# Another order of TensorE's calls in one step of a strided-attention kernel

## The reference, cut to what matters

```python
xn = layernorm(x)                                   # x: 4 x 2048 x 256, float32
q, k, v = heads(xn @ q_w), heads(xn @ k_w), heads(xn @ v_w)      # 16 heads of 16
q = q * sigmoid(unity_scale)
scores = q @ k.T / sqrt(16)
allowed = (j % 4 == 0) | (abs(i - j) <= 8)          # key j for query i
attn = softmax(where(allowed, scores, -inf))
linear = fp8_round(xn) @ weight_fp8.T + bias
out = x + (attn @ v) @ o_w + o_b + linear
```

## Time and profile before

| | us |
|---|---|
| median of 3 runs | 1435.28 (1432.79 to 1437.56) |
| profiled execution | 1432.67 |
| its span, first to last instruction | 1430.9 |
| TensorE busy | 1333.4 (93%) |
| VectorE busy | 1072.3 (75%) |
| ScalarE busy | 824.4 (58%) |
| GpSimd busy | 265.6 (19%) |
| steps with units and scores, 343.03 to 1306.12 | 963.1 |

### The profile page before, as it was taken

How to read it: one execution, slowest core, us unless ns; L and a number is a source line. 1 busy time by engine, 2 the same in 40 slices (tenths; PEclk the granted TensorE clock), 3 DMA queues, 4 the chain that set the end, 5 groups by cost and what they waited for, 6 DMA issues and landing times.

```text
span 1430.9 us, 29098 instructions
## 1 busy us (share of the span) xinstructions
PE 1333.4 (93%) x9792; PEld 635.7 (44%) x9792; DVE 1072.3 (75%) x2583; ACT 824.4 (58%) x1524; POOL 265.6 (19%) x382
## 2 busy tenths in 40 slices
PE   6689888979999999999999999999999999999996
PEld 3466666623434334434334443444344344444385
DVE  7999999777777777767767776777677777777222
ACT  2333333306777667767666776767677667776800
POOL 5543333420111111111111111111111111111100
PEclk9899999958999999999999999999999999999998
DMA  5566666962354444435353544444353525443258
GB/s 179 166 182 182 176 189 196 236 147 41 95 109 102 100 103 110 107 92 103 96 106 92 111 103 97 100 103 109 95 108 95 109 88 117 103 101 94 71 175 289
DMA packets 209060, 178.08 MB, mean 124 GB/s; under 512 B 49808, under 2 KB 185616, under 8 KB 207376
## 3 DMA queue, kind: packets, MB, share of 16 engines
q1 hardware_dynamic: 201168, 168.20, 46.2%
q10 hardware_dynamic: 7744, 7.87, 1.7%
HBM read 106.93 MB, written 69.07 MB: 123 GB/s over the span
## 4 chain that ended last, share of the span: by engine, by line
PE 64%; DMA 10%; issue 2%; ACT 1%; DVE 1%; ACTq 0%; POOL 0%; DVEq 0%; POOLq 0%
PE ps_attend L919 17%; PE ps_attend L934 15%; PE ps_attend L895 15%; DMA q_op<-negmax_dram 9%; PE ps_attend L941 5%; PE ps_attend L903 3%; PE ps_attend L900 3%; PE ps_attend L976 3%; PE ps_attend L920 3%; ACT probs L813 1%; DVE masked L866 1%; DMA q_op<-attn_dram 1%; PE ps_attend L892 1%; ACT out_rows L785 0%; ACT probs L818 0%
## 5 line engine op out<-in xcount | busy, mean ns | idle before, releaser
L866 DVE CUSTOM_DVE_ANT_0 masked<-ps_attend,max_mask 128x620 bf16<-128x620 f32 x1024 | 774.5, 801 | 255.5 <-PE ps_attend L920 252.2
L813 ACT ACTIVATE probs<-ps_attend 128x512 f32<-128x512 f32 x1024 | 572.3, 600 | 280.2 <-PE ps_attend L895 278.7
L919 PE MATMUL ps_attend<-k_op,q_op 96*128 96x512 bf16 x1024 | 404.7, 395 | 26.3 <-issue 15.3
L895 PE MATMUL ps_attend<-q_op,k_op 99*128 99x512 bf16 x1024 | 393.2, 386 | 9.6 <-DMA q_op<-negmax_dram 6.2
L934 PE MATMUL ps_attend<-probs,v_op 128*32 128x512 f32 x2048 | 275.8, 611 | 0.1
L919 PEld LDWEIGHTS ps_attend<-k_op,q_op 96*128 96x128 bf16 x1024 | 100.2, 98 | 298.4 <-DVE peak L866 254.8
L920 PE MATMUL ps_attend<-k_op,q_op 96*128 96x108 bf16 x1024 | 219.0, 214 | 0.0
L690 POOL CAST negmax<-peak 128x16 bf16<-128x16 f32 x64 | 12.6, 196 | 887.9 <-DVE peak L866 887.9
L895 PEld LDWEIGHTS ps_attend<-q_op,k_op 99*128 99x128 bf16 x1024 | 99.1, 98 | 157.2 <-ACT probs L818 23.2
L818 ACT ACTIVATE probs<-ps_attend 108x512 f32<-108x512 f32 x256 | 145.9, 601 | 0.6 <-PE ps_attend L903 0.5
L920 PEld LDWEIGHTS ps_attend<-k_op,q_op 96*128 96x128 bf16 x1024 | 102.0, 100 | 46.2 <-issue 2.4
(11 more groups left out here) (70 smaller groups left out, 1074.9 us busy)
## 6 DMA issues: line engine op xcount, KB each, us to landing
k_op<-k_parts_dram SPq DMA_DIRECT2D x96, 256.0 KB, 4.7
q_op<-q_parts_dram SPq DMA_DIRECT2D x384, 64.0 KB, 2.7
v_dram<-v_sb SPq DMA_DIRECT2D x64, 256.0 KB, 3.3
share_rows<-shares_dram SPq DMA_DIRECT2D x64, 256.0 KB
attn_dram<-out_rows SPq DMA_DIRECT2D x64, 256.0 KB, 4.2
v_op<-v_dram SPq DMA_DIRECT2D x48, 288.0 KB
q_parts_dram<-qk_parts SPq DMA_DIRECT2D x48, 256.0 KB, 4.0
k_parts_dram<-qk_parts SPq DMA_DIRECT2D x48, 192.0 KB, 2.2
```

The costliest lines, as they stand in the source:

```text
L813: ins = nc.scalar.activation(probs[:, r, h], ps_s[st.bank(kind)], ACT.Exp)
L866: nc.vector.tensor_tensor_reduce(masked[:, i % 2], ps_u[i % 2][:, 0:UNIT], keep["max_mask"][:, mask], 1.0, -3e38, ALU.add, ALU.max, peak[: ...
L895: ins = nc.tensor.matmul(bank, k[0:KM, h * S + r * P:h * S + (r + 1) * P], q[:, h], start=True, stop=True)
L919: nc.tensor.matmul(ps_u[i % 2][:, 0:NS], cols, k[0:KR, h * S:h * S + NS], start=True, stop=True)
```

## The change

`entries` no longer computes the order of the entries from rounds; a tuple `SCORES` has it written out. TensorE's `body` no longer loops over rounds; it names its 16 units, 20 scores, NM and five weightings one by one. Their number, shapes and operands are the same.

Before, a step is

```diff
+SCORES = (
+    ("far", 0, 0), ("far", 0, 1), ("far", 0, 2), ("negmax",), ("far", 0, 3),
+    ("far", 1, 0), ("far", 1, 1), ("far", 1, 2), ("near", 0), ("far", 1, 3),
+    ("near", 1), ("near", 2), ("far", 2, 0), ("far", 2, 1), ("far", 2, 2),
+    ("far", 2, 3), ("far", 3, 0), ("far", 3, 1), ("far", 3, 2), ("near", 3),
+    ("far", 3, 3),
+)
 def entries(s):
-    out = []
-    for r in range(ROUNDS - 1):
-        if r == 1 and -1 <= s and s + 1 < STEPS:
-            out.append(("negmax",))
-        if 0 <= s < STEPS:
-            out += [("far", r, h) for h in range(HG // 2)]
-            out += [("near", h) for h in range(HG) if max(h, 1) == r]
-            out += [("far", r, h) for h in range(HG // 2, HG)]
-    return out
+    return [kind for kind in SCORES
+            if (-1 <= s and s + 1 < STEPS if kind == ("negmax",) else 0 <= s < STEPS)]
...
             def body(st):
-                for r in range(ROUNDS - 1):
-                    if ("negmax",) in st.entries() and r == 1:
+                def ahead(i):
+                    if st.exists(2):
+                        unit(st, i // HG, i % HG)
...
+                def weigh_last(r):
+                    if st.exists(-1):
+                        weigh(st, -1, r)
+
+                def weigh_own(r):
+                    if st.exists():
+                        weigh(st, 0, r)
+
+                far(0, 0)
+                ahead(0)
+                ahead(1)
+                far(0, 1)
+                far(0, 2)
+                weigh_last(3)
+                ahead(2)
+                maxima()
+                far(0, 3)
...
```

More of the change, by code:

```diff
@@ L947, in body @@
             def body(st):
-                for r in range(ROUNDS - 1):
-                    if ("negmax",) in st.entries() and r == 1:
-                        score(st, ("negmax",))
[L951 to L962, removed]
+                def ahead(i):
+                    if st.exists(2):
+                        unit(st, i // HG, i % HG)
@@ new lines, in far, with near, maxima @@
+                def far(r, h):
+                    if st.exists():
+                        score(st, ("far", r, h))
+                def near(h):
+                    if st.exists():
+                        score(st, ("near", h))
+                def maxima():
+                    if ("negmax",) in st.entries():
+                        score(st, ("negmax",))
+                def weigh_last(r):
+                    if st.exists(-1):
+                        weigh(st, -1, r)
+                def weigh_own(r):
+                    if st.exists():
+                        weigh(st, 0, r)
@@ new lines, in body @@
+                far(0, 0)
[7 more added lines that the diff above has]
+                far(0, 3)
+                far(1, 0)
+                ahead(3)
+                far(1, 1)
+                ahead(4)
+                weigh_last(4)
+                ahead(5)
+                far(1, 2)
+                ahead(6)
+                near(0)
+                far(1, 3)
@@ new lines, in body @@
+                ahead(7)
+                near(1)
+                ahead(8)
+                near(2)
+                far(2, 0)
+                ahead(9)
+                far(2, 1)
+                ahead(10)
+                weigh_own(0)
+                far(2, 2)
+                ahead(11)
+                far(2, 3)
+                ahead(12)
+                far(3, 0)
+                weigh_own(1)
+                far(3, 1)
+                ahead(13)
+                far(3, 2)
+                near(3)
@@ L964, in project @@
+                ahead(14)
+                far(3, 3)
+                ahead(15)
+                weigh_own(2)
             def project(j, n):
```

## The result

The changed kernel took 1400.39 us (median of 4, 1399.23 to 1401.51), the kernel before 1434.03 (1429.71 to 1437.56): a ratio of 0.9767, 95% interval 0.9737 to 0.9796. Forecast were 1402, in a range of 1392 to 1416. The profiled executions are 1432.67 and 1401.24 us, 31.4 apart, and what follows divides these.

A forecast was written before the change was run, and what follows sets the result against it. TensorE's order was taken to set the pace, with 0.50 us of late starts per plain step of 15.73. Terms 30.0 - 1.2 + 3.0 + 1.5 = 33.3 us gave 1402 us on the median's footing, range 1392 to 1416.

The forecast's parts named there:

- The three stalls: Late starts of F13 (0.18), U11 and U15 (0.16 each) in a plain step all go: 30.0 us over 60 steps.
- tight units: U6, U8 and U10 come with margins of 0.01 to 0.05; charged 0.02 a step, -1.2 us.
- two new pairs: A unit behind a unit (U0, U1) and a weighting behind a unit (W4, W0, W2): same price as before.
- The load before F00: F00's wait for the load of the maxima shrinks from 0.45 to about 0.3 in 20 steps: +3.0 us.
- `copy_out` behind W4: ScalarE stands at the copy until W4 is done; its pause of 0.6 is covered, so no cost.
- The end: Last two steps, without units: the new order spreads weightings that stood behind four F in a row, +1.5 us.
- The turns: The six turns of TensorE's hardware loop keep their instructions: 0, by +-3 us in all.
- new small stalls: Rival: a weighting behind a unit, or U6, U8 and U10, start late, 0.2 a step: 1413 us, chance 0.14.
- the DMA chain moved with the copy: Rival was a chain standing still: share_rows and load land as before relative to F33, F00 waits 0.9: 1414 us, chance 0.10.
- F00's waits didn't go wholly: Rival was no wait before F00 at all, +9 us instead of +3: 1396 us, chance 0.08.
- nothing was slower: Rival was store of the shares landing in 5 us, F00 waiting 2.6: 1464 us; chance 0.06 including other mechanisms.
- L895 on ScalarE's exponential gone: Sign in the list of waits: this line, a wait on ScalarE's exponential, disappears.

The follow-up runs named there:

- a single call moved: Kernel before with W0 moved one place earlier, between U7 and F13: 1415.2 us, ratio 0.9897 to the kernel before.
- A third order: Another order of TensorE's calls, with NM directly behind W4' and F00 behind W3', against the kernel before: 1392.39 us, ratio 0.9734.
- the experiment: Changed kernel with the load of share_rows issued as four loads of 32 rows: 1391.84 us, 7.0 less than the changed kernel beside it.
- repeated changed kernel: The changed kernel measured once more, unedited, on the second chip: 1398.82 us, ratio 0.9779 to the kernel before.
- either of its halves undone: Changed kernel with its five weightings put back to about the rounds' ends: 1484.9 us; with near entries N0 to N2 put back together: 1466.01 us.

## Why the prediction was right

*What bounds.* TensorE's own order, with three late starts in each step. Shown: in the plain steps after, all starts are on time, and a single call moved took away a single stall.

*Plain step 15.23 forecast, 15.28 measured.* The three stalls went whole: 30.0 us forecast for them, and starts read to 0.001 instead of 0.01 give 0.51, so 30.9. The 1.2 charged for tight units was not needed: U6, U8 and U10 came in time by their 0.01 to 0.05. Instead a term was missing, 0.09 a step for NM's lead-in behind a unit; the prediction took it that no call's price depends on its neighbours, named two new pairs and overlooked this third, which was the one that cost. A third order without it took 15.18. Other pairs came out cheaper by 0.04 together. Net: 28.8 forecast, 27.6 measured.

*The load before F00.* +3.0 forecast, +4.7 measured. That the load stands behind `share_rows` is shown by the experiment. `share_rows` was issued 2.70 behind the store of the shares (532.56 to 535.26) instead of 3.89, and 4.6 behind the store before it (530.67), close to the 4.4 forecast; that this store sets the landing of the shares fits the rows and was not tried:

```profile
530.67 0.42 SPq L750 DMA_DIRECT2D attn_dram<-out_rows  x1
532.56 0.34 SPq L755 DMA_DIRECT2D shares_dram<-shares  x1
533.71 0.56 SPq L760 DMA_DIRECT2D sums_dram<-out_rows  x1
534.31 0.91 SPq L75 DMA_DIRECT2D k_op<-k_parts_dram  x2
535.26 0.58 SPq L764 DMA_DIRECT2D share_rows<-shares_dram  x1
```

F00 was late 12 times by 0.3 on average, not 20 times by 0.3: the size was right, the count was not, and "two of four steps" became one of five. What the prediction didn't have is U0's 0.15 behind a late F00: TensorE's sequencer had stood at F00's wait, and the trace has three register operations for U0's waits behind it, 0.1 us apart (543.42, 543.53, 543.62), before U0 at 543.73. In the repeated changed kernel's trace all this lateness is 6.0 us and not 4.9, so of the 4.7 about one is within chance.

The rule of the Trainium skill ("DMA: Bandwidth & Descriptors", queues, rings and completion order), by which the engines take turns between the queues, is not borne out for this pair: on a queue of its own the load moved nothing for 5.5 us while the other queue did, and it landed 1.6 us sooner once `share_rows` went out in four parts; whether its packets had reached the engines by then, the trace doesn't tell. The same page's section on why a DMA increments its semaphore by 16 says that a transfer runs on the largest number of engines, up to 16, that divides the slowest dimension of both its sides; `share_rows` has 4 there on its DRAM side, and the DMA share of 0.26 in its stretch agrees.

*`copy_out` behind W4.* Nothing, as forecast: ScalarE waited 26.6 us in all for W4 (60 times) and no score was late for it.

*The ends and the turns.* The end was forecast at +1.5, between 0 and 4, and gave 3.4; all six traces with the changed kernel's order there have the same 35.8 us, so this is the order's. The turns were forecast at 0 by 3 either way, and the profiled pair shows -3.7, just outside. The start was to keep its time and took 1.4 more, but in the repeated changed kernel's trace it is 0.3 more. The first part's 1.1 is no effect of the change. So 33.3 forecast, 31.4 measured between the profiled executions, 33.6 between the medians: that the sum comes so close is in part luck, since misses of 1 to 4 us in six terms largely cancel. The 27.6 of the plain steps, most of the gain, does not depend on that.

*The rivals.* No new small stalls at the units; the DMA chain moved with the copy; F00's waits didn't go wholly; nothing was slower. That the changed kernel with either of its halves undone is slower than the kernel before, the prediction didn't say.

*The signs.* Plain step, the 0.14 of W0, W2 and W4 behind a unit, and the copy (about 0.5 earlier after F00, 0.6 forecast) came as named. "L895 on ScalarE's exponential gone" did not: that line grew sevenfold, under the name of weight loads behind weightings. It was the wrong sign to name, as the prediction itself said that such totals are no cost.

## What to carry to other kernels

Where an engine feeds several short queues, its order is to be walked call by call with starts read from a trace: here that gave the plain steps of six new orders to 0.05 us in five and 0.14 in one, two slower ones among them. Here either kind of call put back lost more than both together had won. And when the engine is over nine tenths busy, the rest lies in what its order can't reach: a small load behind a large transfer that uses four of sixteen DMA engines (7 us here, with the transfer spread and cut in four), and the turns of a hardware loop (27 us).

## What the runs showed of the hardware that had not been expected

- A matmul whose weights have 48 columns (NM) starts 0.09 us late behind a bf16 one with 128, as the float32 weightings with 32 do, and its successor 0.11 late; behind a weighting it starts on time. Its weight load begins with it and not under its predecessor.
- Turns of TensorE's loop cost between 2.3 and 7.3 us each in these kernels: 2.1 to 3.2 us without instructions, and the rest by how long the clock stood at half behind them. Over six turns that was 6.8 us in the kernel with the weightings undone, 41.0 in the one with the near entries undone, and 20.5 to 27.3 in the others. The other engines' written-out programs and TensorE's 64 written-out steps ran without such gaps.
- The 256 KB of `share_rows` landed 6.0 us after issue in the median as one transfer over four engines; in four transfers spread over all, each landed 3.3 us after its own issue, and the last 4.9 us after the first one's.
